# A transformer layer on one core: router and decay logits of four groups side by side, outputs in two halves, row scatters split up within a step

## The reference, cut to what matters

```
xn  = layernorm(x)
q, k = xn @ Wq, xn @ Wk          # 4 heads of 32
v, g = xn @ Wv, xn @ Wg          # 4 heads of 64
gk  = log_sigmoid(xn @ Wgk + bgk) / 16
o   = chunked gated linear attention (q, k, v, decay gk), state carried along a sequence
o   = o * rsqrt(mean(o*o) + eps) * gnorm_w * g * sigmoid(g)
attn = o @ Wo
e   = argmax(xn @ gate_w); w = softmax(xn @ gate_w)[e]      # 8 experts, one per token
ffn = w * (gelu(xn @ w1[e] + b1[e]) @ w2[e] + b2[e])        # 128 -> 512 -> 128
out = x + attn + ffn
```

## Time and profile before

| | |
|---|---|
| median of 3 runs | 447.07 us (446.12 to 447.21) |
| the profiled execution, its own time | 444.98 us |
| its span, first to last instruction | 443.3 us |
| PE busy | 419.6 us (95%) |
| DVE / ACT / POOL busy | 308.5 / 310.6 / 287.4 us |
| mean granted clock of TensorE | 0.988 |
| chain that ended last | PE 63%, ACT 14%, POOL 5% |

### The profile page before, as it was taken

One profiled execution on the slowest core, in us unless ns is written; L12 is line 12 of the kernel. 1 busy time (PEld: TensorE's weight loads), 2 busy tenths in 40 slices (PEclk: granted clock), 3 DMA queues, 4 the chain that ended last, 5 costly groups with the idle time before them and its releaser, 6 DMA issues.

```text
span 443.3 us, 12400 instructions
## 1 busy us (share of the span) xinstructions
PE 419.6 (95%) x3074; PEld 366.9 (83%) x3075; DVE 308.5 (70%) x930; ACT 310.6 (70%) x952; POOL 287.4 (65%) x245
## 2 busy tenths in 40 slices
PE   8997999999999999999999999989999999999990
PEld 6665788888778877877877888889999999999990
DVE  5985798897756757657667567866766776866760
ACT  3688888687867867767678678746666766666660
POOL 8530253456776776767767763417888888888884
PEclk9999899999999999999999999999999999999996
DMA  9725378336456343454454444004554555555540
GB/s 239 190 83 170 140 235 302 139 116 163 134 145 175 91 130 114 120 154 154 134 160 134 117 132 134 12 29 72 70 68 63 71 62 65 69 66 64 74 37 0
DMA packets 59096, 51.29 MB, mean 116 GB/s; under 512 B 7200, under 2 KB 51392, under 8 KB 59072
## 3 DMA queue, kind: packets, MB, share of 16 engines
q1 hardware_dynamic: 45936, 42.07, 34.0%
q0 software_dynamic: 12272, 8.54, 14.0%
q10 hardware_dynamic: 864, 0.40, 0.4%
HBM read 33.14 MB, written 18.30 MB: 116 GB/s over the span
## 4 chain that ended last, share of the span: by engine, by line
PE 63%; ACT 14%; POOL 5%; issue 5%; another core or an unknown queue 5%; DVE 4%; ACTq 1%; DVEq 0%; POOLq 0%
PE psA L905 14%; PE psVG L893 14%; ACT E L1069 8%; PE psO L746 7%; PE psVG L716 5%; POOL rms L544 4%; PE psA L729 4%; PE psQK L704 3%; PE psO L631 2%; PE psO L759 2%; DVE ms L1384 2%; PE psT L770 2%; PE psT L778 2%; ACT sq L1078 2%
## 5 line engine op out<-in xcount | busy, mean ns | idle before, releaser
L578 POOL DMA_INDIRECT out_dram<-yw,sidx x71 | 114.9, 1618 | 29.0 <-issue 9.1
L544 POOL TENSOR_TENSOR rms<-msn,neg_half 128x8 f32<-128x8 f32 x32 | 53.2, 1661 | 42.8 <-DVE msn L1388 42.8
L1069 ACT ACTIVATE E<-gcB,ngc 128x128 f32<-128x128 f32 x256 | 78.5, 400 | 0.0
L746 PEld LDWEIGHTS psO<-v_sb,pr 128*128 128x128 f32 x512 | 64.6, 191 | 14.7 <-issue 12.0
L746 PE MATMUL psO<-v_sb,pr 128*128 128x64 f32 x512 | 66.5, 273 | 8.5 <-DVE og L1428 4.7
L550 POOL DMA_INDIRECT sorted_rows<-x_all,pos_i x64 | 63.3, 989 | 17.1 <-issue 17.1
L537 POOL TENSOR_SCALAR_AFFINE_SELECT E<-E 128x1024 f32<-128x1024 f32 x32 | 35.5, 1111 | 51.5 <-ACT E L1069 51.0
L1384 DVE TENSOR_REDUCE ms<-sq 128x8 f32<-128x512 f32 x32 | 21.9, 686 | 62.1 <-ACT sq L1078 62.0
L1078 ACT ACTIVATE sq<-psO 128x512 f32<-128x512 f32 x32 | 19.1, 596 | 41.9 <-remote 40.0
L1416 DVE TENSOR_TENSOR pr<-psA,E 128x512 f32<-128x512 f32 x64 | 40.9, 680 | 0.0
L905 PE MATMUL psA<-xT_all,v_sb 128*128 x288 | 38.2, 276 | 0.4 <-issue 0.4
(11 more groups left out here) (191 smaller groups left out, 957.2 us busy)
## 6 DMA issues: line engine op xcount, KB each, us to landing
gcB<-decay_rows SPq DMA_DIRECT2D x32, 512.0 KB
sorted_rows<-blank SPq DMA_DIRECT2D x12, 396.0 KB, 5.6
xg<-sorted_rows SPq DMA_DIRECT2D x71, 66.0 KB
x_all<-in_L_attn_x_dram SPq DMA_DIRECT2D x16, 256.0 KB, 5.3
out_dram<-res SPq DMA_DIRECT2D x32, 128.0 KB
eqB<-decay_exp_rows SPq DMA_DIRECT2D x32, 64.0 KB
w1b<-in_L_ffn_w_dram SPq DMA_DIRECT2D x8, 256.0 KB
xT_all<-in_L_ffn_w_dram SPq DMA_DIRECT2D x32, 64.0 KB
```

The lines of the kernel that those rows point to most:

```text
L544: nc.gpsimd.tensor_tensor(rms[:], msn[:], neg_half[:, 0:2 * H], ALU.pow).then_inc(rms_ready, 1)
L578: nc.gpsimd.indirect_dma_start(out=out_rows, out_offset=bass.IndirectOffsetOnAxis(ap=sidx[j][:], axis=0), in_=yw[j][:], in_offset=None, bo ...
L746: last = nc.tensor.matmul(psO[:, k * HV + h * DV:k * HV + (h + 1) * DV], pr[:, h // 2, k * SEQ + h % 2 * P:k * SEQ + (h % 2 + 1) * P], v_s ...
L1069: last = nc.scalar.activation(E[j][:, k, h * P:(h + 1) * P], gcB[j][:, k * H + h, :], ACT.Exp, bias=ngcf[:, bass.ds((s * 2 + k) * H + h, 1)])
```

## The change

It has three parts and a reordering.

1. `wr_pad` is one set of 32 columns (12 used, 20 zeros) in place of four sets of 160. `logits(S)` now makes all four groups of a super at once: for each q a matmul with 32 stationary columns that writes the 32 partitions 32q to 32q + 31 of the bank, each with `start` and `stop` of its own. It needs all four groups copied. The lists of TensorE, ScalarE and VectorE in the preamble are put in another order to match: fewer, later logits, transposes ahead of them, `decay_logits(0)` ahead of statistics batch 5, batch 7 behind `choose(0)`, `copy_lg(3)` ahead of `copy_qk(0, 1)`.
2. `outputs` writes psO in two halves of 64 partitions: each matmul becomes two with 64 stationary columns, in turn lower and upper half. The moving operand stays, so there are twice as many matmuls.
3. `place_rows(t)` places one tile. In step s the first of three now comes behind the mask and a wait for `qk_ready` of s + 2 (TensorE's projection of step s + 1), ahead of `rms_step`; the second behind `rms_step`; the third behind a wait for `oT_ps_ready` of s (the transposes at the end of TensorE's step s), which puts it ahead of the next step's mask.

The diff, with little context:

```diff
@@ -140,7 +140,7 @@
         wr_sb = sb("wr_sb", [P, NL])
-        wr_pad = sb("wr_pad", [P, GT, P + LS])
+        wr_pad = sb("wr_pad", [P, LS])
         wo_raw = sb("wo_raw", [P, 2, D])
@@ -544,26 +544,32 @@
 
-            def place_rows(s):
-                pool.sem_inc(tick, 1)
-                for t in range(s * 3, min(s * 3 + 3, TILES)):
+            def place_rows(t):
+                if t < TILES:
+                    pool.sem_inc(tick, 1)
                     nc.gpsimd.indirect_dma_start(out=sorted_dram, out_offset=bass.IndirectOffsetOnAxis(ap=pos_i[:, t:t + 1], axis=0),
...
             def step(s):
+                t = (s - PLACE_FROM) * 3
                 if s < SEQS:
                     mask_dec(*divmod(s, 2))
+                if s == PLACE_FROM:
+                    pool.wait_ge(dve_late, LATE)
+                    pool.wait_ge(sort_cleared, CLEARS * 16)
+                if s >= PLACE_FROM and t < TILES:
+                    pool.wait_ge(qk_ready, s + 2)
+                    place_rows(t)
                 if s >= 1:
...
                     finish_band()
-                if s == PLACE_FROM:
-                    pool.wait_ge(dve_late, LATE)
-                    pool.wait_ge(sort_cleared, CLEARS * 16)
-                if s >= PLACE_FROM:
-                    place_rows(s - PLACE_FROM)
+                if s >= PLACE_FROM and t + 1 < TILES:
+                    place_rows(t + 1)
+                    pool.wait_ge(oT_ps_ready, s)
+                    place_rows(t + 2)
 
@@ -620,18 +626,18 @@
 
-            def logits(g):
-                S, q = divmod(g, GT)
-                pe.wait_ge(xT_copied, g + 1)
-                if g == 0:
+            def logits(S):
+                pe.wait_ge(xT_copied, (S + 1) * GT)
+                if S == 0:
                     pe.wait_ge(wr_padded, 1)
-                if q == 0 and S >= 2:
+                if S >= 2:
 
                     pe.wait_ge(lgT_copied, S)
-                last = nc.tensor.matmul(ps_lgT[S][:], wr_flat[:, q * P:(q + 1) * P], xT_flat[:, g * GT * P:(g + 1) * GT * P],
-                                        start=(q == 0), stop=(q == GT - 1))
-                if q == GT - 1:
-                    last.then_inc(lgT_ps_ready, 1)
+                for q in range(GT):
+                    g = S * GT + q
+                    last = nc.tensor.matmul(ps_lgT[S][q * LS:(q + 1) * LS, :], wr_pad[:], xT_flat[:, g * GT * P:(g + 1) * GT * P],
+                                            start=True, stop=True)
+                last.then_inc(lgT_ps_ready, 1)
 
@@ -743,9 +749,11 @@
                 for h in range(H):
-                    last = nc.tensor.matmul(psO[:, k * HV + h * DV:k * HV + (h + 1) * DV], pr[:, h // 2, k * SEQ + h % 2 * P:k * SEQ + (h % 2 + 1) * P],
-                                            v_sb[j][:, k, h * DV:(h + 1) * DV], start=(k == 0 and h == 0), stop=(k == 1 and h == H - 1),
-                                            skip_group_check=True)
+                    for c in range(2):
+                        t = k * SEQ + h % 2 * P + c * P // 2
+                        last = nc.tensor.matmul(psO[c * P // 2:(c + 1) * P // 2, k * HV + h * DV:k * HV + (h + 1) * DV], pr[:, h // 2, t:t + P // 2],
+                                                v_sb[j][:, k, h * DV:(h + 1) * DV], start=(k == 0 and h == 0), stop=(k == 1 and h == H - 1),
+                                                skip_group_check=True)
                 return last
@@ -756,7 +764,9 @@
                 pe.wait_ge(qe_ready, s + 1)
-                nc.tensor.matmul(psO[:, HV:2 * HV], qe[j][:], S_sb[:], start=False, stop=False, skip_group_check=True)
+                for c in range(2):
+                    nc.tensor.matmul(psO[c * P // 2:(c + 1) * P // 2, HV:2 * HV], qe[j][:, c * P // 2:(c + 1) * P // 2], S_sb[:],
+                                     start=False, stop=False, skip_group_check=True)
                 own_half(i, j, 1).then_inc(o_ready, 1)
@@ -798,7 +808,6 @@
             xT_flat = xT_all[:].rearrange("p s n -> p (s n)")
-            wr_flat = wr_pad[:].rearrange("p a n -> p (a n)")
 
@@ -808,47 +817,38 @@
             transpose_x(2)
+            transpose_x(3)
+            transpose_x(4)
             logits(0)
-            transpose_x(3)
+            centre_w()
+            transpose_x(5)
+            logits_back(0)
+            transpose_x(6)
+            transpose_x(7)
+            transpose_x(8)
             logits(1)
-            logits(2)
-            transpose_x(4)
-            logits(3)
-            centre_w()
-            for g in range(4, 7):
-                transpose_x(g + 1)
-                logits(g)
-            logits(7)
-            logits_back(0)
-            transpose_x(8)
             transpose_x(9)
...
             transpose_x(10)
-            logits(8)
-            transpose_x(11)
-            logits(9)
             pe.wait_ge(w_split, 3)
...
             proj_vg(0, 0)
+            transpose_x(11)
             transpose_x(12)
+            logits(2)
             pe.wait_ge(pool_consts, POOL_CONSTS)
...
             decay_sums(0)
-            logits(10)
             transpose_x(13)
-            logits(11)
             transpose_x(14)
             transpose_x(15)
-            logits(12)
-            logits(13)
             logits_back(2)
-            logits(14)
-            logits(15)
+            logits(3)
             pe.wait_ge(lgT_copied, 2)
...
             scores(0, 0)
+            logits_back(3)
             proj_qk(0, 1)
-            logits_back(3)
             proj_vg(0, 1)
@@ -972,9 +972,7 @@
                 act.wait_ge(first_consts, 6)
-                for q in range(GT):
-                    last = nc.scalar.copy(wr_pad[:, q, 0:NL], psVG[:, 1, 0:NL])
-                last.then_inc(wr_padded, 1)
+                nc.scalar.copy(wr_pad[:, 0:NL], psVG[:, 1, 0:NL]).then_inc(wr_padded, 1)
 
@@ -1107,41 +1105,39 @@
             pad_wr()
-            copy_xT(2)
+            for g in range(2, 5):
+                copy_xT(g)
             act.wait_ge(xT_copied, 1)
             split_hi(0, 0)
-            copy_xT(3)
-            copy_xT(4)
             copy_lgT(0)
             w_high()
+            copy_xT(5)
+            copy_lg(0)
             split_hi(0, 1)
-            for g in range(5, 8):
+            for g in range(6, 9):
                 copy_xT(g)
             copy_lgT(1)
-            copy_lg(0)
-            copy_xT(8)
+            copy_xT(9)
             copy_lg(1)
-            copy_xT(9)
             copy_xT(10)
             log_gate(0)
+            copy_qk(0, 0)
             copy_xT(11)
-            copy_qk(0, 0)
             copy_xT(12)
...
             copy_b1()
-            copy_xT(13)
             copy_lgT(2)
-            copy_xT(14)
-            copy_xT(15)
+            for g in range(13, 16):
+                copy_xT(g)
             tanh(0, 0)
...
             exp_dec(0, 0)
+            copy_lg(3)
             copy_qk(0, 1)
-            copy_lg(3)
             log_gate(1)
@@ -1491,12 +1487,11 @@
             statistics(4)
-            statistics(5)
             dve.wait_ge(small_loaded, SMALL * 16)
             decay_logits(0)
+            statistics(5)
+            decay_gates(0)
             statistics(6)
-            decay_gates(0)
-            statistics(7)
             take_q0()
@@ -1504,6 +1499,7 @@
             choose(0)
+            statistics(7)
             make_gate(0, 0)
...
             decay_k(0, 0)
```

## The result

The changed kernel took 436.96 us (median of four runs, 434.74 to 438.18) beside 447.14 us for the kernel before in the same set of runs: a ratio of 0.974, 95% interval 0.970 to 0.978. It is 2.6% faster there; 426 us were forecast. The time is inside the range of 414 to 440 us, 11 us above the forecast.

The account below looks back on a forecast made before the run. TensorE bounds attention and preamble, but TensorE reports delivered late during placing scatters lose 14.8 us in 20 steps. Gains of 3.5 + 13.8 + 4.0 = 21.3 us from 444.98 give 423.7, stated as 426 us towards the median; range 414 to 440.

Parts of the forecast that it names:

- A scatter step of 7.45 us: Attention steps with placing scatters: 8.14 falls to about 7.45 us, 20 x 0.69 = 13.8 us gained.
- GpSimd's own circle: GpSimd's list with first (A), second (B), third (C) scatter, mask, `rms` and hold sets the step: 7.35 to 7.5 us.
- what is queued behind each wait: Check of moved scatters: mask 0.6 us late, covered by 1.8 us before TensorE wants `pr`.
- `on` ... 2.0 us of cover: nothing: First scatter (A) delays `rms` 1.3 us; `on` ends 2.0 us before the transposes need it, so no cost.
- Hold about 1.0: Wait ahead of the third scatter: transposes' report delivered late behind the second, about 1.0 us in GpSimd's list.
- single scatters hold nothing back: Rival: reports not or only briefly delayed, steps go to TensorE's 6.95 us, 416 us in all; chance 0.15.
- The outputs in halves: Output matmuls: halves side by side take 1.6 us, 0.5 less; 0.4 counted in 10 steps, 4.0 us.
- GpSimd's circle hides it: Outputs in halves: no gain counted in the 20 scatter steps, as GpSimd's list sets their length.
- The preamble: 3.5 us: Router logits in quarters: 9 us less TensorE work, 3.5 us gained, first `pr` at about 35.8 instead of 39.3.
- A sign of being wrong that came: Scatter steps: a new ScalarE or VectorE wait of over 1 us for a TensorE report in each step.
- The holds only change their victim: Rival: `vg_ready` and `a_ready` late by 1 us without slack, steps of 7.8 us, 433 us; chance 0.12.
- Column halves only in part together: Rival: output matmuls take 2.5 us, steps of 7.7 us, 438 us in all; chance 0.12.

Follow-up runs that it names:

- set 3: Runs on one chip where the kernel before took 430.49 us: changed kernel 436.68 us (1.011), without its two new waits 417.94, with the scatters' move undone 414.62.
- The scatter without B: Changed kernel without the second placing scatter of each step (21 of 64 tiles not placed): 437.4 us, a single run.
- slow-before: Sets of runs in which the unchanged kernel before took 445.3 to 448.0 us.
- quick-before: Sets of runs in which the unchanged kernel before took 431.7 and 430.5 us.

## Why the prediction was right or wrong

- **The sign, for the set it was made on: right.** The late reports of the earlier trace rows are what the kernel before lost in its scatter steps there, and splitting the row of three scatters took the wait before `sq` away. That the sign held was luck in part: in set 3 the same change lost 1.1%, and the prediction didn't ask. Nor does a time inside the wide range speak for the sum: the 20 scatter steps gave 6.0 us where it had 13.8.
- **A scatter step of 7.45 us: wrong, 7.84.** The step that failed is "GpSimd's own circle is C 1.0, mask 1.1, A 1.2, `rms` 1.85, B 1.2, hold about 1.0". The scatter without B shows that B isn't in the circle. From `rms` the circle goes on through VectorE and TensorE (`on`, `qe`, `res`, transposes, 2.1 us) back to C, because the change makes C wait for them. I had written "what is queued behind each wait", but for this one asked only whether mask and `pr` have slack, and not whether what is queued behind C leads back to what C waits for. It does: C, mask, A, `rms`, `on`, the transposes of the same step. "`on` ... 2.0 us of cover: nothing" was true of A by itself; C's wait, its start and the mask had used that cover already. Sum of the error: 20 x 0.39 = 7.8 us.
- **"Hold about 1.0": the size was near, the cause was wrong.** The transposes' report isn't late; the 0.81 us are the scatter's own start behind a wait. No placing scatter of the kernel before stands behind a wait, so its price couldn't be read there; I had priced it by the reports' lateness instead. Nothing was held by the single scatters either: `th` waits 0.3 us and not 0.5 to 0.9. So the condition of the rival "single scatters hold nothing back" came true, and its 416 us did not, since the circle through C's wait is the longer one.
- **The two steps ahead of the 20: missed.** In the earlier trace rows they run at 7.40 with scatters already in them. The circle closes at once, they take 8.2 each: +1.6 us where -0.8 was in the sum, 2.4 us.
- **The outputs in halves: 0.5 us a step, right,** and side by side, as the row halves of the earlier trace rows suggested. Two undisturbed steps gave 1.0 us against 0.8. The Trainium skill, "TensorE: Matmul & The Clock Gate", section "Part 3: Packing small matmuls", says that loads overlap with running matmuls only where the row group differs; by that they would have taken 2.5 us or more, by my estimate. Here 36 passes and their loads took 1.5 us, so for column halves the trace doesn't agree. What I didn't see is that alone they cost time in a slow-before set, since "GpSimd's circle hides it" was thought of for the new order only.
- **The preamble: 3.5 us was too much.** With the halves' share the changed kernel is 3.5 us ahead at the start of the scatters, where this term and six steps of 0.4 made 5.9. The first `pr` came 1.3 us earlier, not 3.5. The decays (`ngc`) were there at 29.21, against 29.36 in the kernel before. TensorE stood for copies and was busy for 2.52 of 5 us, and got 0.66 of its clock in the next 5, a part at 1.2 GHz, in which the decay sums lie:

```profile
20.00:25.00 5.00, 2.52 (x19) 1.22 (x17) 4.64 (x32) 4.09 (x9) 2.40 (x2) 1.00 0.02 3
25.00:30.00 5.00, 3.65 (x16) 3.37 (x16) 2.44 (x12) 2.82 (x7) 1.65 (x1) 0.66 0.06 18
...
23.69 1.07 PE L638 MATMUL psO<-xT_all,wr_pad 128*32 128x512 f32 x8 [2.40 <-ACT xT_all L969]
...
29.21 0.29 DVE L1277 SCALAR_TENSOR_TENSOR ngc<-psT,lnv 128x128 f32<-128x128 f32 x1 [2.43 <-ACT w1b L1023]
```

  VectorE then waited 2.4 us for the decays. The clock was in the range at 0.9 us and not in the sum. It doesn't account for the whole miss: with the full clock there the profile of the logits alone has the first `pr` 2.2 us earlier, not 3.5, and the kernel before has a drop of its own, 0.82 from 40 to 45 us and 0.84 in the next 5, which the changed kernel doesn't have (mean clocks 0.988 and 0.989). By the runs of the logits alone the term was 0 in most executions and 2 in one.
- **A sign of being wrong that came:** a new wait of ScalarE for TensorE of over 1 us, before `qb`, 26.2 us in 17 steps. It isn't a late report (`qb` starts 0.12 us after the last pass for k, at 162.16), but TensorE itself coming late by its wait for `res`: it is the circle seen from ScalarE.
- **Together:** 7.8 + 2.4 + 2.4 us, less the 0.2 gained behind the scatters, make 12.4 of the 12.5 us between 423.7 and the profiled 436.22.
- **The rivals near the measured time.** "The holds only change their victim" had the nearest step (7.8 us; 433 us in all), by another mechanism: it is the wait added by the change, not a delayed report, that took the gain. "Column halves only in part together" had the nearest time, 438 us, but its condition, outputs of 2.5 us, didn't hold, and 440 us, nothing of the hold gone, is near by chance too: the wait before `sq` did go.
- **Not asked at all:** whether the late reports, the base of the 13.8 us, are always there. The kernel before was slow in three of five sets.

## What to carry to other kernels

A wait that is added on one engine must be followed round: list what is queued behind it, what that releases, and see whether the chain ends at the event waited for; if so its length is the new step, whatever slack each piece had alone. Before moving work to avoid a disturbance, measure again in another set of runs whether it is always there, and prefer a version whose time doesn't depend on it: here the same order without waits. And time a part of a change by itself, more than once, when a profile shows a gain in a preamble: the one that was profiled here was 2.6 us quicker than the median of its ten, which showed no gain.

## What the runs showed of the hardware

- An indirect scatter that had to wait starts 0.8 us after its releaser (0.81 behind the transposes, 0.82 behind the projections), while ScalarE starts 0.1 us after the same reports. Behind work it starts after 0.2 to 0.3 us. Only waits for TensorE were seen, so whether another releaser costs the same is open.
- In slow-before sets TensorE's reports come late (`sq` 2.0 us behind the outputs), and TensorE stands 0.2 to 1.1 us between instructions, during and shortly after the issue of a scatter; in a quick-before set neither is seen with the same order of scatters and the outputs in halves. What differs between the sets stays open: it isn't the chip, and within a set it doesn't change. Whether the reports and the standing have one cause is open; no run separates them.
- The same scatter takes 0.96 us, and 1.50 us where VectorE's `on` started 0.1 us before it, in each such step. `msn`, an operation of 0.17 us, takes 1.77 us when the mask starts on GpSimd while it runs, in every second step, and ends with it:

```profile
153.15 1.77 DVE L1384 SCALAR_TENSOR_TENSOR msn<-ms,vpe 128x8 f32<-128x8 f32 x1
...
153.79 1.10 POOL L537 TENSOR_SCALAR_AFFINE_SELECT E<-E 128x1024 f32<-128x1024 f32 x1
```

  It ends at 154.92, the mask at 154.89. So the two engines seem to stand in each other's way; no run separates these two effects.
